# Expert work, state-space scan and last sample of a two-layer transformer kernel in a new order

## What is computed

```python
def _L1_attn_ref(x, ...):                     # the mixer
    xr = x @ in_proj_w + in_proj_b
    x_in, res = xr[..., :256], xr[..., 256:]
    xc = silu(conv_b + sum(shifted(x_in, k) * conv_w[k] for k in range(4)))
    d_raw, Bm, Cm = split(xc @ x_proj_w + x_proj_b, 3)          # 16 each
    delta = softplus(d_raw @ dt_proj_w + dt_proj_b)
    dA, dBx = exp(delta[..., None] * A), (delta * xc)[..., None] * Bm
    h = dA_t * h + dBx_t;  y_t = sum_n(h * C_t)                 # over 512 rows
    return (y + xc * D_skip) * silu(res) @ out_proj_w + out_proj_b

def _L1_ffn_ref(x, ...):                      # the large experts
    combine = scatter(softmax(top_2(x @ gate_w)))
    h = gelu(einsum('td,edf->tef', x, w1) + b1)
    y = einsum('tef,efd->ted', h, w2) + b2
    return einsum('ted,te->td', y, combine)
```

## Time and profile before

| | |
|---|---|
| median of 3 runs | 1411.71 us (1411.7 to 1413.48) |
| the profiled execution | 1414.16 us |
| its span, first to last instruction | 1412.3 us |
| mean granted clock of TensorE | 0.952 of full |
| PE busy | 1207.2 us, 85% |
| DVE busy | 1059.1 us, 75% |
| ACT busy | 865.2 us, 61% |
| POOL busy | 463.0 us, 33% |

### The profile page before, as it was taken

The page is one execution under the profiler, slowest core; times in us unless marked ns, Lnnn a source line. Parts: engine busy times, 40 slices in busy tenths (PEclk is TensorE's granted clock), DMA queues, the critical chain, the costliest instruction groups (busy, mean ns, idle before and its releaser), DMA issues. The chain is left out here.

```text
span 1412.3 us, 19389 instructions
## 1 busy us (share of the span) xinstructions
PE 1207.2 (85%) x6560; PEld 760.0 (54%) x6560; DVE 1059.1 (75%) x2427; ACT 865.2 (61%) x1608; POOL 463.0 (33%) x276
## 2 busy tenths in 40 slices
PE   5974689988998889988898889988899889888697
PEld 4641155645664556645565555555656456545465
DVE  2667977699867997599866997589876998679721
ACT  2635455586647866488557866488655876378342
POOL 0004910096003830077101940059100960038300
PEclk8996589999999999999999999999999999999899
DMA  6102100020002100030001100020000200021000
GB/s 239 69 16 75 45 9 8 29 100 1 16 16 76 45 16 1 16 105 16 16 16 49 72 8 9 16 91 31 16 9 24 105 1 9 1 76 45 8 0 8
DMA packets 18499, 53.22 MB, mean 38 GB/s; under 512 B 4961, under 2 KB 5849, under 8 KB 18017
## 3 DMA queue, kind: packets, MB, share of 16 engines
q1 hardware_dynamic: 16112, 43.40, 9.2%
q0 software_dynamic: 1280, 4.20, 1.0%
q10 hardware_dynamic: 1008, 4.38, 0.8%
HBM read 45.40 MB, written 2.38 MB: 34 GB/s over the span
## 5 line engine op out<-in xcount | busy, mean ns | idle before, releaser
L1413 DVE TENSOR_TENSOR_SCAN probs_T<-bank,probs_T 128x512 f32<-128x512 f32 x256 | 304.8, 1212 | 36.6 <-ACT bank L1006 23.6
L436 POOL TENSOR_TENSOR probs_T<-step_space,probs_T 128x1024 f32<-128x1024 f32 x120 | 282.0, 2359 | 0.0
L557 PEld LDWEIGHTS bank<-w_w,hidden 128*128 128x128 f32 x2048 | 244.3, 192 | 65.6 <-issue 54.7
L545 PE MATMUL bank<-hT,w_w 128*128 128x512 f32 x512 | 257.8, 624 | 25.0 <-ACT hidden L862 25.0
L557 PE MATMUL bank<-w_w,hidden 128*128 128x128 f32 x2048 | 247.3, 276 | 8.8 <-issue 7.5
L862 ACT ACTIVATE hidden<-bank,w_b 128x512 f32<-128x512 f32 x256 | 171.4, 686 | 124.6 <-PE bank L545 124.0
L434 POOL TENSOR_TENSOR probs_T<-step_space,probs_T 128x512 f32<-128x512 f32 x16 | 22.9, 1451 | 680.9 <-DVE step_space L1403 680.9
L935 ACT ACTIVATE probs<-bank,row_neg 128x128 f32<-128x128 f32 (+3 forms) x256 | 135.0, 529 | 152.2 <-DVE row_neg L1264 135.8
L1006 ACT ACTIVATE bank<-step_space,a_neg 128x512 f32<-128x512 f32 x256 | 168.4, 684 | 69.0 <-DVE probs_T L1413 57.6
L639 PE MATMUL bank<-k_pad,q_lat 128*128 128x512 f32 (+3 forms) x512 | 185.7, 449 | 5.2 <-DMA k_pad<-xc 5.2
L1264 DVE TENSOR_REDUCE row_neg<-bank 128x1 f32<-128x128 f32 (+3 forms) x256 | 123.4, 486 | 85.5 <-PE bank L641 83.2
(11 more groups left out here) (180 smaller groups left out, 1574.1 us busy)
## 6 DMA issues: line engine op xcount, KB each, us to landing
probs_T<-b_rows_dram SPq DMA_DIRECT2D x64, 512.0 KB, 3.6
w_w<-in_w_dram ACTq DMA_DIRECT2D x2, 2048.0 KB, 13.3
k_pad<-xc SPq DMA_DIRECT2D x64, 64.0 KB, 2.0
x_in<-in_x_dram POOLq DMA_DIRECT2D x8, 256.0 KB, 3.2
gate<-gate_rows_dram SPq DMA_DIRECT2D x1, 2048.0 KB, 7.4
out_dram<-x_out POOLq DMA_DIRECT2D x8, 256.0 KB, 2.8
step_space<-in_wmod_dram SPq DMA_DIRECT2D x1, 768.0 KB, 5.3
probs_T<-in_wqT_dram SPq DMA_DIRECT2D x1, 512.0 KB, 4.1
```

The lines of the kernel that those rows point to most:

```text
L436: ins = nc.gpsimd.tensor_tensor(inject[:, n % 3, :, :], u[:], row.unsqueeze(1).to_broadcast([P, DH, T]), ALU.mult)
L545: mm(hid1_bank(n)[:], w["w1"][:, n // C1, n % C1 * P:(n % C1 + 1) * P], hT[3][:], start=True, stop=True).then_inc(hid1_mm.sem, 1)
L557: ins = mm(bank[OUT1_BANK[e]][:, t * P:(t + 1) * P], hidden[:, (e * C1 + c) % (2 * C1), t * P:(t + 1) * P], w["w2"][:, e * C1 + c, :], sta ...
L1413: v.tensor_tensor_scan(state[:, n % 2, c, :], decay(DH * n + c)[:], inject[:, n % 3, c, :], 0.0, ALU.mult, ALU.add).then_inc(st_ok.sem, 1)
```

## The change

1. **Ahead of the scan, ACT and PE.** Chunks 2 and 3 of expert 2 (`early(2, (2, 3))`) move from behind proj to the input projections: PE makes one ahead of the first and one between the second and third; ACT runs their gelus between `xi` and `res_gate` and then loads the silu table by hand. Behind `xc` ACT loads the exp/log table instead of the gelu table. PE spreads the output tiles of expert 1: two ahead of x_proj, one behind it, one behind the delta projection. PE's wait for `split` and `dt_z` moves from ahead of expert 2's outputs to the start of `scan`.
2. **DVE.** The split is made of five instructions instead of seven, by subtractions that write bf16; its last two come behind u. Expert 1's adds move behind `dt_in`, and u of a half comes directly behind the half's delta.
3. **The scan.** New tables for hidden chunks, output tiles, gelus (groups of 4, 2, 3, 3, 2, 3, 3 behind decays 2, 7, 11, 15, 19, 23, 27 in place of 2, 3, 3, 2, 4, 3, 3 behind 2, 5, 11, 14, 19, 24, 28) and adds.
4. **The tail.** Skip and gate of the last sample come ahead of `finish` of the one before. PE makes two hidden chunks ahead of the router. Output tiles alternate between banks 0 and 1 (the last expert's in 1 and 4), so that an expert waits for the adds of the one before the last. The last expert's adds, the final two operations and the store run in two halves of two tiles.

```diff
 # PE, main
                 layernorm(b, 2, MISC, (gates_ok.sem, gates_ok.at(b, 1)))
+                early(2, (2,))
                 h_wait(b, 2)
                 for c in range(2 * DH):
+                    if c == 2:
+                        early(2, (3,))
                     if c >= 2:
                         pe.wait_ge(in_out.sem, in_out.at(b, c - 1))
...
-                early(1, out=True)
+                early(1, out=True, tiles=(0, 1))
...
-                early(2, (2, 3))
+                early(1, out=True, tiles=(2,))
...
+                early(1, out=True, tiles=(3,))
                 early(3, (0, 1))
-                pe.wait_ge(split_ok.sem, split_ok.at(b, 1))
-                pe.wait_ge(dt_z.sem, dt_z.at(b, DH))
-
                 early(2, out=True)
 # PE, tail
             last_sum(B - 1)
+            pe.wait_ge(out1_add.sem, out1_add.at(B - 2, E * NT + 1))
             mixer_out_mm(B - 1)
 
             expert_head(B - 1, 0)
+            h_wait(B - 1, 3)
+            for n in range(2):
+                hid1(B - 1, n)
             expert_head(B - 1, 1)
-            for n in range(C1):
+            for n in range(2, C1):
                 hid1(B - 1, n)
 # PE, out1
                     pe.wait_ge(hid1_act.sem, hid1_act.at(b, (e + 1) * C1))
-                    if e >= 1:
+                    if e >= 2 and tail:
+
+                        pe.wait_ge(out1_add.sem, out1_add.at(b, (e - 1) * NT + 1))
+                    elif e >= 1 and not tail:
 # ACT, iteration
                 for c in range(2 * DH):
+                    if c == DH:
+                        early(2, (2, 3))
+                        nc.scalar.preload_act_table_set("silu_and_others")
...
-                nc.scalar.preload_act_table_set("gelu_and_others")
+                nc.scalar.preload_act_table_set("natural_log_exp_and_others")
                 act.wait_ge(pr_mm.sem, pr_mm.at(b, 1))
                 f(proj[:], bank[MISC][0:PR, :], ACT.Identity, bias=w["x_proj_b"][:]).then_inc(pr_out.sem, 1)
-                early(2, (2, 3))
-                nc.scalar.preload_act_table_set("natural_log_exp_and_others")
 # DVE, iteration
-                early(1)
 
                 dve.wait_ge(pr_out.sem, pr_out.at(b, 1))
+                mid, low = slice(L, 2 * L), slice(2 * L, 3 * L)
                 link(cp(split[:], proj[0:3 * BC, :]))
-                for lo, hi in ((L, 2 * L), (2 * L, 3 * L)):
-                    link(tt(part[lo:hi, :], proj[lo:hi, :], split[lo:hi, :], ALU.subtract))
-                    link(cp(split[lo:hi, :], part[lo:hi, :]))
-                lo = 2 * L
-                link(tt(part2[lo:lo + L, :], part[lo:lo + L, :], split[lo:lo + L, :], ALU.subtract))
-                cp(split[lo:lo + L, :], part2[lo:lo + L, :]).then_inc(split_ok.sem, 1)
+                mark(tt(split[mid, :], proj[mid, :], split[mid, :], ALU.subtract))
+                link(tt(part[low, :], proj[low, :], split[low, :], ALU.subtract))
                 for c in range(DH):
                     dve.wait_ge(chain_a.sem, chain_a.at(b, c + 1))
                     ts(dt_in[:, c, :], bank[HID0_BANK[c]][:], w["dt_b"][:, c:c + 1], None, ALU.add).then_inc(dt_z.sem, 1)
+                early(1)
                 for c in range(DH):
-
                     dve.wait_ge(dt_z.sem, dt_z.at(b, c + 1))
                     dve.wait_ge(dt_l.sem, dt_l.at(b, c + 1))
                     stt(delta[:, c, :], dt_in[:, c, :], 0.0, dt_log[:, c, :], ALU.max, ALU.add).then_inc(delta_ok.sem, 1)
-                for c in range(DH):
                     dve.wait_ge(delta_ok.sem, delta_ok.at(b, c + 1))
                     tt(u[:, c, :], delta[:, c, :], xc[:, c, :], ALU.mult).then_inc(u_ok.sem, 1)
+                link(cp(split[low, :], part[low, :]))
+                tt(split[low, :], part[low, :], split[low, :], ALU.subtract).then_inc(split_ok.sem, 1)
 # DVE, end
             scan_end(B - 1, True)
+            tail = linker(dve, chain_tail, B - 1)
+            mixer_end(B - 1, 0, tail)
             finish(B - 2)
-            tail = linker(dve, chain_tail, B - 1)
-            for k in range(2):
-                mixer_end(B - 1, k, tail)
+            mixer_end(B - 1, 1, tail)
...
+            for half in range(2):
+                tiles = slice(2 * half, 2 * half + 2)
+                for t in range(2 * half, 2 * half + 2):
+                    add_expert(B - 1, E * NT - NT + t, tail=True)
...
+                tt(x_out[:, tiles, :], x_mid[:, tiles, :], expert_out[:, tiles, :], ALU.add).then_inc(last_half, 1)
 # POOL, end
-            store(B - 1)
+            for half in range(2):
+                pool.wait_ge(last_half, half + 1)
+                pool.dma_start(out_rows[B - 1, :, 2 * half:2 * half + 2, :], x_out[:, 2 * half:2 * half + 2, :]
+                               ).then_inc(last_sent, 16)
+            pool.wait_ge(last_sent, 32)
 # the tables
-SCAN_HIDDEN = {0: (14, 16), 1: (16, 18), 3: (18, 19), 4: (19, 21), 5: (21, 22), 6: (22, 23), 7: (23, 24),
-               8: (24, 26), 10: (26, 29), 12: (29, 32)}
-SCAN_OUTPUT = {1: (12, 13), 2: (13, 16), 4: (16, 17), 5: (17, 19), 7: (19, 20), 8: (20, 23), 9: (23, 24),
-               10: (24, 25), 11: (25, 28), 13: (28, 30), 14: (30, 32)}
-SCAN_GELU = {2: (12, 14), 5: (14, 17), 11: (17, 20), 14: (20, 22), 19: (22, 26), 24: (26, 29), 28: (29, 32)}
-SCAN_ADD = (0, 4, 8, 10, 13)
+SCAN_HIDDEN = {0: (14, 17), 1: (17, 18), 2: (18, 19), 3: (19, 20), 4: (20, 22), 5: (22, 23), 6: (23, 24),
+               7: (24, 26), 8: (26, 27), 9: (27, 28), 10: (28, 31), 12: (31, 32)}
+SCAN_OUTPUT = {0: (12, 14), 1: (14, 15), 2: (15, 16), 5: (16, 19), 6: (19, 20), 7: (20, 21), 8: (21, 22),
+               9: (22, 24), 10: (24, 25), 11: (25, 26), 12: (26, 28), 13: (28, 31), 14: (31, 32)}
+SCAN_GELU = {2: (12, 16), 7: (16, 18), 11: (18, 21), 15: (21, 24), 19: (24, 26), 23: (26, 29), 27: (29, 32)}
+SCAN_ADD = (0, 5, 7, 10, 13)
```

More of the change, by code:

```diff
@@ L205, in build @@
         OUT1_BANK = (1,) * EARLY_E + (6,) * (E - EARLY_E)
+        TAIL_BANK = tuple((e % 2,) * NT for e in range(E - 1)) + ((1, 1, 4, 4),)
         def hid1_bank(n):
@@ L618, in main, with early @@
             def main(b, behind, ahead, ending):
-                def early(e, chunks=(), out=False):
+                def early(e, chunks=(), out=False, tiles=range(NT)):
                     if behind:
@@ L625, in early @@
                         if out:
-                            for t in range(NT):
+                            for t in tiles:
                                 out1(b - 1, e * NT + t)
```

33 lines of the change are left out of this document (22 added, 11 removed).

## The result

After the change the kernel takes 1390.05 us, the median of four runs (1384.17 to 1395.5), against 1412.39 of the kernel before (four runs, 1411.7 to 1413.48). The ratio is 0.984 [0.980, 0.987]. The forecast of 1387.2 lies 2.9 us under it, and the range holds it. The runs fall on two values, near 1384.4 and near 1395.5; that is the start of the program and not the change, as the first experiment shows. The profiled run took 1384.17 us with a span of 1382.4.

What follows compares the result with a forecast made beforehand. The prediction saw a relay between engines bounding the stretch ahead of each scan, and DVE bounding the scan. Savings of 1.4 + 10.0 + 10.8 + 2.3 = 24.5 us from 1411.71 gave 1387.2, range 1384.5 to 1390.5 (1382.5 to 1393.5 with rivals).

Steps and rivals of the forecast that it cites:

- Ahead of the scan: From proj to the first scan instruction: 1.43 us saved in each of seven samples, 10.0 in all.
- The first sample: The sample without expert work: shorter split and u behind its delta save 1.4 us.
- The scan: Seven scans: idle falls from 24.3 to 10.9 us; less 2.6 for clock drops, 10.8 us saved.
- The rule for the groups: In the scan: each ACT gelu group, four gelus taking 6.05 us, is set against DVE's work before the next decay's use.
- The 1.36 us ahead of the fourth scan instruction: Start of each scan: DVE idle expected because the first group of four gelus makes the next decay late.
- rival A: Scan starts: the clock stays up in every new scan, 2.6 us less, 1384.4 us; chance 0.17.
- the 24.3: DVE idle, in us, counted in seven scans of the kernel before, at the seventh scan instruction and later.
- The clock: PE at scan starts: idle of about 1.8 us, clock drops in three scans, costing 2.6 us.
- The tail: Behind the last scan: earlier skip and gate, reordered router, alternating banks and halves save 2.3 us, bounds 0.5 and 4.
- Rival C: Stretch ahead of the scan gives 0.5 instead of 1.43 us, u's early half or gelu cover failing: 1393.5; chance 0.12.
- Rival D: Scan's second to seventh groups: PE's in-order queue makes the third gelu late; slower, 1418.7 us at 0.75 each; chance 0.05.
- rivals A, B and C: Besides rival A and Rival C, B: a clock drop at every scan start meeting the first group, 1392.8 us; chance 0.11.

Runs made afterwards that it cites:

- the first experiment: The changed kernel run again without any edit: 1386.95 us (six runs), ratio 0.983.
- The delayed POOL: Changed kernel with POOL's first product held back until the split is done: 1391.47 us, ratio 0.984.
- the last experiment: Changed kernel with the split's remainder in PSUM, u behind both deltas and the tail's router ahead of the hidden chunks: 1378.09 us, ratio 0.975.
- everything but the scan's order: Changed kernel with the four scan tables of the kernel before: 1411.95 us, ratio 1.001.
- the early cast and subtraction: Changed kernel with the split's last cast and subtraction ahead of the first delta: 1402.64 us, ratio 0.991.

## Why the prediction came out right, and where it was not

The time lies in the range and 2.9 us from the forecast, but the agreement is partly luck: two large terms are wrong by 14.7 and 15.4 us and cancel.

- **Ahead of the scan, 10.0 forecast, a loss of 4.7 measured.** Up to the first half of u each step came as worked out. Ln ends 4.81 us behind the cast (forecast 4.8), delta starts at +4.47 (4.45), the gelus are hidden with 0.25 us to spare (0.2), the first decay starts at +6.51 (6.5). The step that failed is "u 768.77 to 769.45 (0.68 each, as in the earlier trace rows)" and "cast and subtraction to 770.53": those durations were read where POOL still stood idle as each began, and the new order puts u's second half and the last subtraction beside the two halves of POOL's first product. 0.95 us each, 1.9 of the 2.1 that are missing. The delayed POOL shows that little else was mis-sized in that sum: without overlap DVE is done at +8.36, for 8.23. The question asked there was who is late next; what was not asked is who runs at the same time. The kernel before shows it, if one looks behind the 2.87 us of the earlier trace rows, of which the prediction took half (1.43) for each product. The first, which starts beside u's second half, takes 1.65 us, the second, alone, 1.26 (the row of the first below). The Trainium skill, SBUF — State Buffer, Who interferes with whom, has this case: a VectorE instruction with two SBUF inputs and a GpSimd one that reads SBUF exclude each other for a whole instruction. The traces agree: 1.63 us beside POOL, 0.68 alone, 0.69 from PSUM. By it the two instructions would have been seen beforehand.

```profile
770.21 1.65 POOL L434 TENSOR_TENSOR probs_T<-step_space,probs_T 128x512 f32<-128x512 f32 x1 [84.75 <-DVE step_space L1403]
```

- **The first sample, 1.4 forecast, 0.0 measured:** the same cause for most of it. Its relay grows from 9.03 to 10.29 us, its scan shrinks from 54.40 to 53.15 as its one wait of 1.08 goes. With nothing held, in the last experiment, its relay is 8.42, so 1.9 of the 2.7 that are missing are the hold; for the other 0.8 no run shows the cause.
- **The scan, 10.8 forecast, 26.2 measured.** The rule for the groups holds: the group of four takes 6.06 us from load to next decay (6.05), idle of 0.11 in all at the later groups (0.19 forecast). Off are three sizes. The 1.36 us ahead of the fourth scan instruction is absent, 9.5 over seven samples, because DVE itself came 2.1 us late by the step above: the decay is ready at +15.19 as forecast (+15.16), DVE wants it at +15.87 (forecast +13.8). That much is the same time booked in another place, and no luck; when DVE is made quick, 0.41 us of it come back. Next the clock: no drop in any scan, 2.6 us (rival A, given 0.17). The last 3.3 are small: 1.1 of short waits of before that I left out of the 24.3, and 2.4 (0.34 per sample) because DVE's instructions overlap each other more, less 0.2, as the short new waits come to 1.6 and not 1.4. Back to back, a scan instruction starts 0.08 us before the one ahead of it has ended (760.14 against 760.22 in after); one that has waited does not. So a wait costs a little more than its idle time, and the prediction left that out.
- **Taken together**, cast to end of scan, the forecast without drops was 68.6 us per sample (8.25, and 62.47 less 3.65 of idle plus 1.55) and 68.90 was measured, from 72.15. Of the mechanism, the decays level again stand, and so does the earlier Ln; the relay as a whole got longer and not shorter. Of the two places where I put the gain one gave all of it.
- **The clock.** The forecast put an idle of 1.8 us into every scan start and drops in three scans. The idle is there (1.82 us), the drops are not. The rows at hand, 1.72 without and 2.38 with a drop, bracketed it, and it fell to the lower side; "some, not all" had no row of its own. That it can happen was shown only later: 3.05 us of idle brought a drop in two of seven scans.
- **The tail, 2.3 forecast, 1.9 measured.** Skip and gate start 1.32 us sooner behind the last read product, just as forecast; at the end of hT 1.04 of it is left. Behind hT the reordered router loses 2.07 us (from 7.70 between the start of ACT's hT and the transposes to 9.77) for 1.83 forecast. From the transposes to the end, with the alternating banks, the halves and the two stores, 2.95 us are won (64.53 to 61.58) for 2.8 forecast. Only this last part is steady: 61.57 to 61.80 in all eleven traces that have it. The part ahead of the transposes moves by 1.8 us between traces of one tail code, so the tail's gain is between 1.8 and 3.6 us against the one trace of before, and its closeness to 2.3 says little.
- **Rival C** was the nearest of the losing cases and had the right place, but the wrong reasons (u's early half, the gelu cover), and not the size: minus 0.68 where it had plus 0.5. Rival D does not occur: in after's fifth scan the third gelu waits for PE for 0.63 or 0.64 us in each group of three or four, which is the wait that the forecast's times for these groups hold already, and DVE's idle time in the later groups is 0.11 in all.
- **The comparison with the median.** The prediction subtracted from the median of three runs that lay within 2 us. The new kernel's runs lie 11 us apart, which the three times of before did not show; eleven runs of the kernel before do (1408.54 to 1418.88). That the median of this set came within 2.9 us of the forecast was luck too.
- **Slips in the sums.** Three drops of 0.9 us are 2.7, not 2.6, and by the prediction's own terms rivals A, B and C come to 1384.6, 1393.0 and 1393.7. None of them bears on the outcome.

## What to carry to other kernels

An instruction's duration belongs to its neighbours: before a VectorE instruction with two SBUF operands is moved in an estimate, look what GpSimd does at the new time, and take one operand from PSUM, or the order that has them apart, where they meet. Lost time of this kind stands in the duration column and not among the waits, so compare the mean of the same form in both traces before trusting a group whose idle time has fallen. And where ACT changes tables inside a loop that needs it regularly, size each group against the slack of the buffers that it feeds: that one reordering, 20.8 us alone where the whole change gave 23.4, needed nothing but the group's own durations.

## What the runs showed of the hardware

- A DVE instruction of 32 partitions is held by POOL as long as one of 128: the 32x512 subtraction goes from 0.68 to 1.63 us, the 128x512 product from 0.69 to 1.64, and even the cast with its one SBUF input from 0.42 to 1.38. With its input in PSUM the cast is not held. POOL pays too, 1.65 and 1.49 us for a product of 1.26.
- From PSUM the 32x512 cast takes 0.69 us against 0.42 from SBUF; 0.27 us is the price of being free of POOL.
- The two profiled executions of the changed kernel differ by 11.2 us in span, of which 9.1 lie ahead of the first sample's cast of proj (112.7 or 121.9 us) and 1.8 in its relay, with PE at 1.2 GHz for 13.7 us and for 30.7 us up to 113 us. All later scans agree to 0.05 us.
- PE's clock stayed at full over each of seven scan starts with an idle of 1.82 us. It fell in all seven behind 3.56 us (everything but the scan's order), in six of seven behind 2.38 us with 1.72 us just ahead of it (the kernel before), and in two of seven behind 3.05 us (the early cast and subtraction). So the length of the idle time alone does not tell, and why one scan in seven of the kernel before had no drop is open. The Trainium skill, TensorE: Matmul & The Clock Gate, What's actually happening, lets the clock fall after an idle stretch only. At the scan starts the runs agree in that: no drop stands there without one. At the program's start there is a drop that does not fit: with everything but the scan's order, the rows show PE busy without a break (its ends are modelled), for 2.3 us of it with 20 matmuls of eight columns, and the clock is at half behind that:

```profile
32.30:35.60 3.30, 3.30 (x29) 3.07 (x28) 0.72 (x2) 1.02 (x4) 0.00 (x0) 1.00 0.00 0
35.70:39.00 3.30, 3.30 (x13) 2.14 (x12) 1.74 (x9) 2.12 (x8) 0.76 (x1) 0.50 0.15 46
```
